# Edge loop: ScalarE's copy of the turned runs between the scalings of the two tiles' old rows

## What is computed

```python
r = concat(node[src], node[dst], edge) @ Wr.T + br
q = node @ Wq.T + bq;  k = r @ Wk.T + bk;  v = r @ Wv.T + bv
a = einsum('ehd,ehd->eh', q[dst], k) / 8
ae = exp(a - segment_max(a, dst)[dst])
out = segment_sum(v * ae / segment_sum(ae, dst)[dst], dst)
```

## Time and profile before

| | |
|---|---|
| median of 3 runs | 1622.1 us (1619.85 to 1623.33) |
| profiled execution | 1626.55 us |
| its span in the profile | 1624.8 us, 27304 instructions |
| TensorE matmuls busy | 1551.1 us (95%), 7334 |
| TensorE weight loads busy | 1202.1 us (74%) |
| VectorE busy | 1256.3 us (77%), 3141 |
| ScalarE busy | 1054.6 us (65%), 3706 |
| GpSimd busy | 694.3 us (43%), 722 |
| mean granted clock of TensorE | 0.984 of full speed |
| HBM traffic over the span | 208 GB/s |

### The profile page before, as it was taken

One profiled execution on the slowest core, in us unless ns is written; L12 is line 12 of the kernel. 1 busy time (PEld: TensorE's weight loads), 2 busy tenths in 40 slices (PEclk: granted clock), 3 DMA queues, 4 the chain that ended last, 5 costly groups with the idle time before them and its releaser, 6 DMA issues. The chain is left out here.

```text
span 1624.8 us, 27304 instructions
## 1 busy us (share of the span) xinstructions
PE 1551.1 (95%) x7334; PEld 1202.1 (74%) x7334; DVE 1256.3 (77%) x3141; ACT 1054.6 (65%) x3706; POOL 694.3 (43%) x722
## 2 busy tenths in 40 slices
PE   7999898999999999999999999999999999899996
PEld 6786676777777777777777777777777777777673
DVE  5866664887788778788788778878877878678878
ACT  3785122677777777777777777777777777567245
POOL 1001123556555555555555565555555565211001
PEclk9999999999999999999999999999999999999997
DMA  6575414666666666666676666666666666175001
GB/s 194 180 247 181 174 67 137 200 215 202 210 208 207 224 211 216 211 199 199 201 239 218 198 218 204 211 206 212 220 208 209 202 201 198 45 236 192 27 14 51
DMA packets 135446, 300.31 MB, mean 185 GB/s; under 512 B 34863, under 2 KB 56502, under 8 KB 135296
## 3 DMA queue, kind: packets, MB, share of 16 engines
q0 software_dynamic: 63600, 180.17, 33.6%
q1 hardware_dynamic: 66512, 107.59, 22.2%
q10 hardware_dynamic: 5184, 10.81, 1.8%
HBM read 271.40 MB, written 66.58 MB: 208 GB/s over the span
## 5 line engine op out<-in xcount | busy, mean ns | idle before, releaser
L1110 ACT ACTIVATE wv<-vv,expd 128x64 f32<-128x64 f32 x1248 | 314.6, 334 | 2.7
L1122 ACT ACTIVATE old<-old,expd 128x64 f32<-128x64 f32 x1232 | 302.1, 334 | 0.0
L1032 POOL DMA_INDIRECT merge<-new,put_id x157 | 162.8, 1037 | 269.2 <-DVE new L1453 236.9
L1882 PE MATMUL psK<-M_hi,efT_hi 128*128 128x512 f32 x628 | 254.3, 405 | 2.8 <-ACT efT_hi L1080 2.8
L1882 PE MATMUL psV<-M_hi,efT_hi 128*128 128x512 f32 x628 | 256.1, 408 | 0.0
L1883 PE MATMUL psK<-M_lo,efT_hi 128*128 128x512 f32 x628 | 250.0, 398 | 0.0
L1883 PE MATMUL psV<-M_lo,efT_hi 128*128 128x512 f32 x628 | 249.5, 397 | 0.0
L1003 POOL DMA_INDIRECT old<-merge,dst_id x157 | 157.8, 1005 | 142.6 <-DMA merge<-new,put_id 116.9
L1096 ACT ACTIVATE expd<-diff 128x32 f32<-128x32 f32 (+1 forms) x79 | 18.1, 229 | 289.3 <-DVE diff L1432 289.3
L1003 POOL DMA_INDIRECT kv<-kv_table,src_id x157 | 162.3, 1034 | 66.1 <-issue 47.8
L1003 POOL DMA_INDIRECT qc<-q_table,dst_id x157 | 155.0, 987 | 54.6 <-issue 46.6
(11 more groups left out here) (323 smaller groups left out, 3334.7 us busy)
## 6 DMA issues: line engine op xcount, KB each, us to landing
first_ef<-in_ef_turned_dram SPq DMA_DIRECT2D x39, 512.0 KB, 5.0
efT<-in_ef_turned_dram SPq DMA_DIRECT2D x39, 512.0 KB
merge<-empty ACTq DMA_DIRECT2D x4, 2640.0 KB, 10.0
rows<-merge SPq DMA_DIRECT2D x40, 256.0 KB, 3.7
row_block<-dst_rows POOLq DMA_DIRECT2D x13, 768.0 KB, 6.1
dst_line<-dst_rows SPq DMA_DIRECT2D x78, 128.0 KB, 2.7
end_line<-end_rows SPq DMA_DIRECT2D x78, 128.0 KB, 4.3
kv_table<-kv_out SPq DMA_DIRECT2D x10, 512.0 KB, 3.2
```

The costliest lines, as they stand in the source:

```text
L1032: pool.indirect_dma_start(out=merge[2 * (p % 2) + u][:, :], out_offset=bass.IndirectOffsetOnAxis(ap=put_id[:, t:t + 1], axis=0), in_=new[p ...
L1110: act.activation(wv[:, u, h * DH:(h + 1) * DH], vv[p % 2][:, u, h * DH:(h + 1) * DH], ACT.Copy, scale=expd[p % 2][:, u, 0, h:h + 1]).then_ ...
L1122: act.activation(rows, rows, ACT.Copy, scale=expd[p % 2][:, u, 1, h:h + 1]).then_inc(old_scaled, 1)
L1882: pe.matmul(out[:, :], efT_hi[b][:, u, c, :], Me_hi[:, c, col:col + D], start=c == 0, stop=False)
```

## The change

Two things are edited on ScalarE, and nothing elsewhere. `scale_old` takes a tile instead of a pair, and the loop calls it for the first tile of pair p-2 ahead of `copy_runs(p-1)` and for the second tile behind it. The instructions and their number stay the same; the tail after the loop is untouched.

```diff
--- before.py
+++ after.py
@@ -1114,12 +1114,12 @@
                     act.wait_ge(summed, t - 1)
                 act.activation(wv_hi[:, u, :], wv[:, u, :], ACT.Copy).then_inc(wv_hi_ready, 1)
 
-            def scale_old(p):
-                for u in range(tiles_of(p)):
-                    act.wait_ge(old_in[p % 2], landed(p))
-                    for h in range(H):
-                        rows = old[p % 2][:, u, h * DH:(h + 1) * DH]
-                        act.activation(rows, rows, ACT.Copy, scale=expd[p % 2][:, u, 1, h:h + 1]).then_inc(old_scaled, 1)
+            def scale_old(t):
+                p, u = t // 2, t % 2
+                act.wait_ge(old_in[p % 2], landed(p))
+                for h in range(H):
+                    rows = old[p % 2][:, u, h * DH:(h + 1) * DH]
+                    act.activation(rows, rows, ACT.Copy, scale=expd[p % 2][:, u, 1, h:h + 1]).then_inc(old_scaled, 1)
 
             def weigh_old(t):
 
@@ -1140,9 +1140,11 @@
                     act.wait_ge(w_in, 16)
                     act.activation(wq_hi[:, p - 30, :], w_raw[:, p - 30, :], ACT.Copy).then_inc(w_high, 1)
                 if p >= 2:
-                    scale_old(p - 2)
+                    scale_old(2 * p - 4)
                 if p >= 1:
                     copy_runs(p - 1)
+                if p >= 2:
+                    scale_old(2 * p - 3)
                 if p == PAIRS - 1:
                     act.wait_ge(w_in, 32)
                     act.wait_ge(ke_done, ET)
```

## The result

The changed kernel takes 1584.6 us (median of 6 runs, 1580.83 to 1589.85) beside 1622.2 us for the one before on the same chip (6 runs). The ratio is 0.9772, 95% interval 0.9754 to 0.9789. On three chips that came in later, kernels with the copy moved forward came out 2 to 8% slower than the kernel before; the changed kernel itself ran on one of them, and lost 6.5%. The experiments come to that.

What follows compares the result with a forecast made beforehand. Bound: ScalarE and VectorE waiting for each other, 14.26 us a pair, with TensorE following at 13.74 undisturbed. Gains of 37.5 us (by period) and 35.6 (by place) gave 36.6: 1622.1 - 36.6 = 1585.5 us, range 1580 to 1600.

Steps and rivals of the forecast that it cites:

- (a): ScalarE's copy starts at 815.6 in place of 817.43, without waiting, as the runs are turned 2.3 us before.
- (e): Four pairs with a 0.62 us weight split on ScalarE, where the wait reaches 1.2 us, also come down to 13.74.
- (f): GpSimd's stores and gathers keep 2.1 us of room a pair; old rows land 1.3 us ahead of the maximum, not 1.8.
- (b): VectorE starts the low part at about 815.8 in place of 817.62, 1.8 us earlier.
- the ring: ScalarE and VectorE waiting for each other once per pair: 14.26 us a round trip, falling to 12.3 with the change.
- (c): The second tile's scalings, now behind the copy, end 0.7 us before VectorE's second row merge wants them; no cost.
- (d): TensorE's wait at the spreading matmuls goes, with 1.5 us to spare; TensorE sets the pair and VectorE waits for it.
- The first rival: Faster by less: late landings of old rows become the rule and GpSimd's ring sets the pair; 1604 us, chance 0.11.
- The way by the period: Gain over the 73 loop pairs from their total time: 1040.54 - 73 x 13.74 = 37.5 us.
- Less gain: A new bound, GpSimd's round with late landings, takes part of the gain: 1592 to 1612, at 1604 us; chance 0.11.
- No change: The wait on the copy hides another of the same size, most likely the second row merge: 1622 us, chance 0.05.
- Slower: VectorE holds up GpSimd's eight indirect transfers per pair, 0.35 us each: 15 us lost, 1637 us; chance 0.04.

Runs made afterwards that it cites:

- the copy behind 12: Copy placed behind 12 of the 16 scalings, where the changed kernel has it behind 8 and the kernel before behind 16: 1586.96 us, ratio 0.9771.

## Why the prediction was right

Forecast 1585.5 us, range 1580 to 1600; measured 1584.6. The profiles of that chip and of chip 11 bear out the steps (a) to (e); (f) was off.

(a), (b) The copy found its runs turned and came earlier by half of the scalings, though with 0.5 us between the two (1068.22 to 1068.74) where I had 2.3: freed of the ring, ScalarE runs ahead of TensorE. The ring's 12.3 us after the change was never measured: with less of TensorE's work another ring of 12.55 us set the pair, the one by the exponentials' high part, whose wait of 0.6 us was in the trace of before and in no step. At 13.74 it made no difference. The test of the copy's ring is the kernel with one scaling moved: 0.24 us per pair. VectorE's wait for the copy fell from 138.0 us to none in the list.

(c) The scalings ended at 1070.81, and the second row merge came half way through the 1.28 us from 1072.09, at 1072.7: 1.9 us of cover where I had 0.7. The low part did not start 0.2 us behind the copy's start but 1.4, since VectorE was by then held up by TensorE. Cover grows when the pair lengthens beyond the ring.

(d) TensorE's wait went, and VectorE's waits on V and K sums are the ones named. The period of 13.74 us, read from three undisturbed pairs at the loop's start, held over 73: 1004.14 us for 1003.

(e) The weight splits cost nothing now: the starts of their four pairs are 13.73 to 13.75 us apart.

(f) is the mis-sized step. GpSimd's issues stayed at 0.957 us, but the landing was taken at 3.7 us, the median of before, and it is 5.6. With the second gather at 1067.25 and that median the rows land at 1072.85, and the maximum wants them at 1073.37: 0.5 us, not 1.3. In 11 of 73 pairs the maximum waits, 9.7 us in all; the row says "issue", but in each of them the last landing of the old rows stands 0.08 us ahead of the maximum, and the spreading matmuls had ended 0.7 us earlier or more. The two longest waits, 2.7 and 2.2 us, lie in the pairs of 14.45 and 13.94, and cost 0.9 us; the other nine cost TensorE nothing. GpSimd's room did not shrink to 2.1 us a pair either: it waits 252.8/71 = 3.6 us for the denominators, as it hardly waits for its stores. The step took SyncE's load to stay where it was against the stores. The first rival had named that it might move, and gave it no price.

*The sum.* 36.4 us in the 73 pairs, for 36.6. The way by the period (37.5) left out the pairs of 14.45 and 13.94, which cost 0.9 us. The profiled executions are 41.6 us apart, as 5.2 more lie outside the 73 pairs, where I had counted nothing and where the cause is open; against that, the profile of before stood 4.4 us above its median and the profile of after 0.3. The two nearly cancel, so that the medians' 37.6 us and the forecast come within 1 us of each other is in part luck. The 36.4 us are not.

*The page on busy share.* The matmuls' busy time would have capped the gain at 20 us; it was 36.4. The warning of the Trainium skill's page "Perfetto Trace Analysis", section "Identifying the Most-Contended Engine", that the matmuls' busy share is no good measure of room, held.

*The rivals.* "Less gain" did not decide here, though its landings did grow and set two pairs. "No change" fell. "Slower" through VectorE's hold on GpSimd's transfers fell as well: 0.957 us per gather with VectorE busy 85% of the stretch. The Trainium skill's page "SBUF — State Buffer", section "Who interferes with whom", has the rule behind it, that VectorE and GpSimd share a port pair under an exclusive lock; the trace shows none of it at 851.51 us of VectorE's work. Most of that work is one kind of instruction, TENSOR_TENSOR, so this says little of the others.

What no step held is that the other side would come true elsewhere, by another mechanism than the one named. The chance for slower of 0.04 was for this chip's kind; of the two chips on which the changed kernel itself ran, it is slower on one. Whether anything in the trace of before could have told is open, as the cause is.

## What to carry to other kernels

When two engines wait for each other once per round, add up the ring and compare it with what an undisturbed round costs the busiest engine; move work that nobody waits for behind the value that closes the ring, and expect the gain to stop at the other engine's period, so a quarter of the way can be worth as much as half. Then look at what the moved signals set off in the DMA queues: a large load that slides from one burst of stores or gathers to the next changes both their landings. And measure a kernel that was brought to a tight pace on more than one chip: with its slack the kernel before lost under 1% where the changed one lost 6.5%.

## What the hardware showed that I had not expected

- One kernel can differ from chip to chip by more than the change brings: 0.977 where the prediction was made (and 0.9771 with the copy behind 12, chip 11), 1.064 on chip 12, while the kernel before stays within 1622 to 1637 us.
- TensorE's semaphores can be raised 4 us behind the matmuls that they ride on, several at once, while later matmuls run on. This was seen in recorded runs only, in traces that lack a part of the signals.
- A wait of some us costs more than itself: in the 73 pairs on chip 12, 90.5 us of idle time came with 54.0 us more for the same matmuls, 116 us of it all at half clock.
- A 512 KB load issued 2.8 us behind the first store of a pair goes with a second store that lands after 5.0 us; issued 4.2 us behind it, that store lands after 2.3 us, and the gathers of old rows after 5.6 us in place of 3.7.
